# Residual and norm offset of a scan stage moved to matmuls with identities

## The chip, the cores and the metric

The kernel runs on one core of a Trainium2 chip. The metric is the device time of one execution in microseconds (us), the median of several runs.

## The reference, cut to what matters

Eight sequences of 512 tokens with 256 features go through a state-space layer and then a mixture of experts. `x` is float32 throughout.

```python
def mamba(x):                                   # 8 x 512 x 256
    x_ssm, x_gate = split(x @ in_w.T + in_b)
    x_conv = silu(causal_conv4(x_ssm) + conv_b)
    Bm, Cm = split(x_conv @ bc_w.T + bc_b)      # 16 states each
    dt = softplus(x_conv @ dt_w.T + dt_b)
    h_n = scan over the tokens: h*exp(dt*A_n) + dt*Bm_n*x_conv     # n = 0..15
    y = (sum over n of h_n*Cm_n + x_conv*D) * silu(x_gate)
    z = (y @ out_w.T + out_b) + x
    return layernorm(z) * ln_g + ln_b
x = layernorm(x + mamba(x))                     # no gain, no offset
x = layernorm(x + moe(x))                       # 8 experts, 4 per token
```

So each sequence has two norms in the scan stage. Between them the first norm's rows are scaled by `ln_g`, and `ln_b` and the old `x` are added.

## The kernel before, in words

The program has three stages: the scan stage with the routing (about 40 to 690 us of the trace, after some setup), the experts, and a last norm. The change touches the first only.

The scan stage runs in rounds, numbered -1 to 9 (`like` in the code; rounds 3 to 6 are a loop). A round has 16 steps, t = 0 to 15, one for each state. In round k several sequences are in flight: part `b` scans sequence k, part `a` prepares sequence k+1 (projection, convolution, softplus, `drive`), part `c` finishes sequence k-1 (output projection, both norms), part `d` routes sequence k-2 and starts to scatter its rows, part `e` scatters the rest of sequence k-3. Rounds 2 to 6 have all of a to d; round 1 has no routing; round 7 has no part a; round 8 has only c, d and e.

Each engine has its own instruction stream in the fixed order of its loop over t (`pe_stage1`, `act_stage1`, `dve_stage1`, `pool_stage1`), and an instruction that waits for a semaphore holds up all behind it on its engine. In step t:

- VectorE multiplies the drive by B (`weigh_inputs`, L894: `p_bu`, 1024 columns) and runs the scan (`scan`, L903: `state`). Other work of the step stands between the two: at t=2 `gate` (L911) and the ranking, at t=5 `take_counts` (L960), at t=9 `residual` (L919, four instructions), at t=11 `softplus_rest` (L867, L870), at t=13 `scan_inputs` (L877), at t=15 `drive` (L885).
- GpSimd multiplies the state of step t-1 by C (`read_state`, L1020: `read`), one step behind the scan. At t=0 it runs `add_offset` (L1053, x + ln_b in place), at t=5 `mean` of the first norm, at t=6 `power`, at t=7 `scale` (L1046, times ln_g), at t=10 `mean` of the second norm (L1030, L1031), at t=12 `power`. It also issues one or two scatters per step (L1062); these stand ahead of the other work of their step. `while_scanning` makes it wait at t=9 for the residual, at t=11 and t=13 for VectorE's softplus work.
- ScalarE computes the decays of step t+2 (`decays`, L693). At t=4 it takes the output projection out of PSUM with row sums (`take_out`, L715), at t=5 and t=11 the variances, at t=6 and t=13 it applies the norms, at t=7 the silu, at t=8 it stores dt and B/C, at t=9 softplus, at t=11 and 12 the gate's projection (`store_in`), which there stands ahead of the decays of the step.
- TensorE adds `read` of step t-2 into `p_y` (`sum_states`, L517), projects `y` at t=3 (`project_out`, L529 to L533), and counts the routed tokens at t=4 (`count`).

Results of TensorE other than `p_y` go through two PSUM banks used in turn, in the order of the list `blocks()`. TensorE waits before a block until the earlier block of that bank has been read (`block`, L465); the reader signals with `bank_read`.

## Time and profile before

| What | Value |
|---|---|
| median of 3 runs | 1407.38 us (1406.16 to 1407.46) |
| the profiled execution | 1408.09 us, of which the span of its trace is 1406.3 us |
| busy over the span | TensorE 1170.1 us, VectorE 1066.2, ScalarE 895.2, GpSimd 791.0 |
| one round in the middle (337 to 412 us) | VectorE 70.1 of 75.0 us, TensorE 62.7, GpSimd 62.5, ScalarE 50.2 |
| the experts and the last norm | from about 690 us to the end |

The 1.8 us outside the span lie before the first and behind the last instruction of the trace. A busy share over the whole span mixes the stages, so the middle row is the one for the scan stage.

### The profile page before, as it was taken

To read this page: it belongs to the slowest core of one execution; us is meant where nothing else is said; L and a number is where in the kernel's file an instruction comes from. 1 tells how busy PE (TensorE), PEld (TensorE's weight loads), DVE (VectorE), ACT (ScalarE), POOL (GpSimd) and SP (SyncE) were. 2 spreads that over 40 slices of the span, in tenths; PEclk is the share of its full clock that TensorE was granted. 3 is DMA by queue.
4 is the path that set the end of the run, shared out by engine and by line. 5 is a ranking of instruction groups with operands and counts; after the bars stand their busy time and mean duration, and the time that the engine had idled before them with its cause. 6 is when DMAs were issued, how large, how long until landed. Compare 5 with 4: busy or idle time off the path is not lost. (4 is left out here: it accounts for less than half of the span.)

```text
span 1406.3 us, 18116 instructions
## 1 busy us (share of the span) xinstructions
PE 1170.1 (83%) x5138; PEld 801.0 (57%) x5138; DVE 1066.2 (76%) x1529; ACT 895.2 (64%) x1549; POOL 791.0 (56%) x567
## 2 busy tenths in 40 slices
PE   7869697979788796761299999999999999999950
PEld 3324252524243433231188888888888888888840
DVE  2999899999999999963177777777777777777743
ACT  4765758494848576422177777776776767776744
POOL 0457568787888888977324444444444444444442
PEclk9899999999999999895599999999999999999985
DMA  2543435444444544424745655565555566555537
GB/s 92 202 151 135 152 120 196 138 170 162 161 159 146 192 153 148 157 73 153 284 140 157 158 156 156 157 155 145 144 143 147 154 159 159 156 155 157 156 40 239
DMA packets 69254, 217.13 MB, mean 154 GB/s; under 512 B 7520, under 2 KB 43232, under 8 KB 56288
## 3 DMA queue, kind: packets, MB, share of 16 engines
q1 hardware_dynamic: 29664, 167.42, 33.0%
q0 software_dynamic: 26880, 36.72, 15.4%
q10 hardware_dynamic: 12672, 12.58, 2.8%
q8 instruction: 12, 0.20, 0.1%
q14 instruction: 26, 0.21, 0.0%
HBM read 165.54 MB, written 51.15 MB: 154 GB/s over the span
## 5 line engine op out<-in xcount | busy, mean ns | idle before, releaser
L517 PE MATMUL p_y<-read,small 128*128 128x512 f32 x512 | 266.6, 653 | 88.6 <-POOL read L1020 88.3
L903 DVE TENSOR_TENSOR_SCAN state<-decay,p_bu 128x1024 f32<-128x1024 f32 x128 | 292.4, 2285 | 13.3 <-DVE p_bu L894 5.1
L1465 POOL DMA_INDIRECT total<-o_v,tok x144 | 267.3, 1856 | 44.0 <-issue 44.0
L517 PEld LDWEIGHTS p_y<-read,small 128*128 128x128 f32 x512 | 98.1, 202 | 236.0 <-POOL read L1020 136.7
L1463 POOL TENSOR_TENSOR scrap<-neg_half 128x1 f32<-128x1 f32 x36 | 14.0, 389 | 356.6 <-ACT o_v L1350 354.0
L693 ACT ACTIVATE decay<-dt,scan_rate 128x511 f32<-128x511 f32 x256 | 164.9, 710 | 22.8 <-DVE state L903 22.6
L1020 POOL TENSOR_TENSOR read<-state,bc 128x1024 f32<-128x1024 f32 x64 | 150.6, 2353 | 29.0 <-DVE p_bu L894 10.7
L1327 ACT ACTIVATE gate_v<-p_g,bias 128x512 f32<-128x512 f32 x144 | 98.3, 683 | 97.8 <-PE p_up L1276 97.7
L1337 ACT ACTIVATE ah<-a_v 128x512 fp32r<-128x512 f32 x144 | 91.2, 633 | 88.9 <-DVE a_v L1411 88.9
L1020 POOL TENSOR_TENSOR read<-state,first_wh 128x1024 f32<-128x1024 f32 x32 | 75.4, 2357 | 81.6 <-DVE p_bu L894 49.8
L1400 DVE TENSOR_SCALAR up_v<-up_v 128x512 f32<-128x512 f32 x144 | 61.3, 426 | 64.2 <-ACT up_v L1330 64.0
L1406 DVE TENSOR_TENSOR al<-a_v,ah 128x512 fp32r<-128x512 f32 x144 | 98.9, 686 | 12.8 <-ACT ah L1337 12.7
L1411 DVE SCALAR_TENSOR_TENSOR a_v<-gate_v,up_v 128x512 f32<-128x512 f32 x144 | 99.8, 693 | 4.9
L1330 ACT ACTIVATE up_v<-p_up,bias 128x512 f32<-128x512 f32 x144 | 98.0, 681 | 0.0
L1020 POOL TENSOR_TENSOR read<-state,first_wl 128x1024 f32<-128x1024 f32 x32 | 75.5, 2358 | 32.8 <-DVE first_raw L870 16.7
L894 DVE TENSOR_TENSOR p_bu<-p_u,bc 128x1024 f32<-128x1024 f32 x64 | 78.9, 1233 | 7.0 <-DVE state L903 0.5
L1292 PE MATMUL p_o<-wh,ah 128*128 128x256 f32 x288 | 82.0, 285 | 1.7 <-DVE al L1406 1.7
L1292 PE MATMUL p_o<-first_wh,ah 128*128 128x256 f32 x288 | 82.0, 285 | 0.0
L1292 PE MATMUL p_o<-wl,ah 128*128 128x256 f32 x288 | 80.6, 280 | 0.0
L1292 PE MATMUL p_o<-first_wl,ah 128*128 128x256 f32 x288 | 80.4, 279 | 0.0
L1292 PE MATMUL p_o<-wh,al 128*128 128x256 f32 x288 | 80.4, 279 | 0.0
L1292 PE MATMUL p_o<-first_wh,al 128*128 128x256 f32 x288 | 80.4, 279 | 0.0
(215 smaller groups left out, 3065.6 us busy)
## 6 DMA issues: line engine op xcount, KB each, us to landing
bc<-bc_rows SPq DMA_DIRECT2D x32, 1024.0 KB
first_raw<-in_w_experts SPq DMA_DIRECT2D x19, 1668.0 KB
raw_w<-in_w_experts SPq DMA_DIRECT2D x18, 1668.0 KB
first_wh<-bc_rows SPq DMA_DIRECT2D x16, 1024.0 KB
first_wl<-bc_rows SPq DMA_DIRECT2D x16, 1024.0 KB
first_rows<-queues SPq DMA_DIRECT2D x19, 544.0 KB
xq<-queues SPq DMA_DIRECT2D x18, 544.0 KB
queues<-read SPq DMA_DIRECT2D x9, 544.0 KB
```

Of the source, the lines that this page charges most:

```text
L517: mm = pe.matmul(p_y[h][:, :], ident[:, :], read[:, t % 4, h, :], start=False, stop=(t == SLOTS - 1))
L693: act.activation(decay[t % AHEAD][:, h, 1:LEN], dt[s.p][:, h, 1:LEN], ACT.Exp, scale=rate[:, h, t:t + 1])\
L894: dve.tensor_tensor(p_bu[:, :].rearrange("p (a b) -> p a b", a=2), p_u[:, :].rearrange("p (a b) -> p a b", a=2), of_state(t, 0), ALU.mult) ...
L903: dve.tensor_tensor_scan(flat(state[t % 4][:, :, :]), flat(decay[t % AHEAD][:, :, :]), p_bu[:, :], 0.0, ALU.mult, ALU.add).then_inc(s_stat ...
L1020: pool.tensor_tensor(read[:, t % 4, :, :], state[t % 4][:, :, :], of_state(t, 1), ALU.mult).then_inc(s_read, 1)
L1292: mm = pe.matmul(to, v[:, i, a * P:(a + 1) * P], w[t.p][:, c:c + D], start=(i == 0 and a % 2 == 0 and m == 0), stop=(i == CH - 1 and m == ...
L1327: act.activation(gate_v[i % 2][:, :], p_g[i % 2][:, :], ACT.Silu, bias=bias[t.p][:, 0, i:i + 1], scale=ALPHA)
L1330: act.activation(up_v[i % 2][:, :], p_up[i % 2][:, :], ACT.Identity, bias=bias[t.p][:, 1, i:i + 1])\
L1337: act.activation(ah[:, i, :], a_v[i % 2][:, :], ACT.Copy).then_inc(s_ah, 1)
L1406: dve.tensor_tensor(al[:, i, :], a_v[i % 2][:, :], ah[:, i, :].bitcast(F32), ALU.subtract).then_inc(s_al, 1)
L1411: dve.scalar_tensor_tensor(a_v[i % 2][:, :], gate_v[i % 2][:, :], TOP, up_v[i % 2][:, :], ALU.min, ALU.mult)\
L1465: pool.indirect_dma_start(total, bass.IndirectOffsetOnAxis(ap=tok[t.p][:, a:a + 1], axis=0), o_v[t.p][:, a, :], None, compute_op=ALU.add). ...
```

## The change

`residual`, on VectorE at t=9, and `add_offset`, on GpSimd at t=0, are gone. In their place TensorE has two new blocks `r0` and `r1` at t=9: for each of the four 128-row tiles it puts into PSUM x through the identity, ln_b through a row of ones (as three bfloat16 parts), and the scaled z through the identity. ScalarE takes these out at t=10 with the row sums, by the same function as at t=4. The second `mean` moves on GpSimd from t=10 to t=11 and now waits for both blocks to be read. `x` stays unchanged in memory, so `project_out` waits for the load of x, and the setup on VectorE splits b_out and ln_b each into three parts, where it split their difference once. GpSimd's wait for the residual at t=9 and ScalarE's wait for it ahead of the load of x are gone.

```diff
@@ blocks
-                + ["dt0", "dt1", "bc", "in2", "in3"] * a)
+                + ["dt0", "dt1", "bc"] * a + ["r0", "r1"] * c + ["in2", "in3"] * a)
@@ pe_stage1
-                pe.matmul(to, ones[0:3, :], b_parts[0:3, :], start=False, stop=False)
+                pe.matmul(to, ones[0:3, :], b_parts[0][0:3, :], start=False, stop=False)
                 if b == 0 and i == 0:
-                    pe.wait_ge(s_offset, s.n + 1)
+                    pe.wait_ge(s_x, 16 * (s.n + 1))
                 mm = pe.matmul(to, ident[:, :], x[:, 2 * b + i, :], start=False, stop=True)
             mm.then_inc(done, 1)
+        def add_residual(r, b):
+            bank, done = block(r, f"r{b}")
+            s = r.s.at(-1)
+            for i in range(2):
+                to = bank[:, i * D:(i + 1) * D]
+                pe.matmul(to, ident[:, :], x[:, 2 * b + i, :], start=True, stop=False)
+                pe.matmul(to, ones[0:3, :], b_parts[1][0:3, :], start=False, stop=False)
+                if b == 0 and i == 0:
+                    pe.wait_ge(s_scaled, s.n + 1)
+                mm = pe.matmul(to, ident[:, :], z[:, 2 * b + i, :], start=False, stop=True)
+            mm.then_inc(done, 1)
@@ (behind from_xc of t == 8)
+                if r.c and t == 9:
+                    add_residual(r, 0)
+                    add_residual(r, 1)
@@ act_stage1
-            after(act, s_residual, s.n)
-        def take_out(r, b):
+        def take_rows(r, which, b):
-            bank, done = full(act, r, f"o{b}")
+            bank, done = full(act, r, f"{'or'[which]}{b}")
             for i in range(2):
                 t = 2 * b + i
+                last = act.activation(z[:, t, :], bank[:, i * D:(i + 1) * D], ACT.Copy,
+                                      accum_out=row_sum[:, which, t:t + 1])
             last.then_inc(done, 1)
@@ (behind the decays of the step)
+                if r.c and t == 10:
+                    take_rows(r, 1, 0)
+                    take_rows(r, 1, 1)
@@ dve_setup
-        steps.then(dve.tensor_tensor(b_rest[:, :], b_out[:, :], ln_b[:, :], ALU.subtract))
+        for of, parts in ((b_out, b_parts[0]), (ln_b, b_parts[1])):
+            steps.then(dve.tensor_copy(b_rest[:, :], of))
+...
@@ dve_stage1
-                if r.c and t == 9:
-                    residual(r)
@@ pool_stage1
+            for b in range(2):
+                bank, n = r.block(f"{'or'[which]}{b}")
+                pool.wait_ge(bank_read[bank], n)
-            if r.c and t == 9:
-                pool.wait_ge(s_residual, r.s.at(-1).n + 1)
-                if r.c and t == 5:
-                    mean(r, 0)
+                if r.c and t in (5, 11):
+                    mean(r, t // 11)
-                if r.c and t == 0:
-                    add_offset(r)
-                if r.c and t == 10:
-                    mean(r, 1)
```

## Rows read from the trace of the kernel before

**Rows 1.** Windows, round 4: PE, PEld, DVE, ACT, POOL busy us; clock, DMA, GB/s.

```profile
337.00:412.00 75.00, 62.73 (x170) 28.76 (x169) 70.12 (x69) 50.21 (x89) 62.53 (x47) 0.95 0.48 164
```

**Rows 2.** Groups by line and shape, 0 to 620 us: busy us, mean ns.

```profile
L919 DVE SCALAR_TENSOR_TENSOR z<-z,x 128x256 f32<-128x256 f32 x28 | 22.6, 858 | 0.0
...
L1053 POOL TENSOR_TENSOR x<-x,small 128x1024 f32<-128x1024 f32 x8 | 16.0, 2004 | 0.0
...
L715 ACT ACTIVATE z<-p_bank 128x256 f32<-128x256 f32 x28 | 10.5, 380 | 34.5 <-PE p_bank L533 34.5
```

**Rows 3.** Timeline, round 4, steps 8 to 10: start, us, engine, tiles, [idle before].

```profile
357.01 1.23 DVE L894 TENSOR_TENSOR p_bu<-p_u,first_wh 128x1024 f32<-128x1024 f32 x1
...
360.84 1.23 DVE L894 TENSOR_TENSOR p_bu<-p_u,first_wh 128x1024 f32<-128x1024 f32 x1
...
361.63 2.37 POOL L1020 TENSOR_TENSOR read<-state,bc 128x1024 f32<-128x1024 f32 x1
...
361.98 2.31 DVE L919 SCALAR_TENSOR_TENSOR z<-z,x 128x256 f32<-128x256 f32 x1
...
368.01 1.23 DVE L894 TENSOR_TENSOR p_bu<-p_u,first_wl 128x1024 f32<-128x1024 f32 x1 [0.47 <-DVE state L903]
```

**Rows 4.** Timeline of round 4, steps 9 to 11, ScalarE's chain.

```profile
361.19 2.56 ACT L693 ACTIVATE decay<-dt,scan_rate 128x511 f32<-128x511 f32 x4
...
366.78 3.70 PE L517 MATMUL p_y<-read,small 128*128 128x512 f32 x8
...
373.36 2.56 ACT L693 ACTIVATE decay<-dt,scan_rate 128x511 f32<-128x511 f32 x4
...
375.24 2.28 DVE L903 TENSOR_TENSOR_SCAN state<-decay,p_bu 128x1024 f32<-128x1024 f32 x1
```

**Rows 5.** Timeline of round 4, steps 11 to 15, GpSimd and what it meets.

```profile
375.42 2.35 POOL L1020 TENSOR_TENSOR read<-state,first_wl 128x1024 f32<-128x1024 f32 x1 [2.28 <-DVE first_raw L870]
...
382.59 1.22 DVE L877 TENSOR_TENSOR dt<-first_raw,rest 128x1024 f32<-128x1024 f32 x1
382.66 1.21 POOL L1039 TENSOR_TENSOR neg_mean<-neg_mean,rstd 128x4 f32<-128x4 f32 x1
...
392.44 1.80 POOL L1062 DMA_INDIRECT queues<-rows,index  x1 [0.17 <-issue]
...
397.79 2.36 POOL L1020 TENSOR_TENSOR read<-state,bc 128x1024 f32<-128x1024 f32 x1
```

**Rows 6.** Timeline, first steps of rounds 4 and 5: TensorE up to the count.

```profile
325.86 1.88 PE L517 MATMUL p_y<-read,small 128*128 128x512 f32 x4
...
345.07 0.19 DVE L960 TENSOR_TENSOR place<-p_bank,base 128x32 f32<-128x32 f32 x1 [0.20 <-PE p_bank L563]
...
401.05 1.88 PE L517 MATMUL p_y<-read,small 128*128 128x512 f32 x4
...
411.48 1.03 PE L474 MATMUL p_bank<-w,y 128*128 128x256 f32 x4
...
413.19 1.03 PE L474 MATMUL p_bank<-w,y 128*128 128x256 f32 x4
```

**Rows 7.** Timeline, VectorE in round -1 and at step 11 of round 1.

```profile
32.79 1.23 DVE L867 SCALAR_TENSOR_TENSOR rest<-rest,expo 128x1024 f32<-128x1024 f32 x1 [14.70 <-ACT rest L672]
...
152.18 2.29 DVE L903 TENSOR_TENSOR_SCAN state<-decay,p_bu 128x1024 f32<-128x1024 f32 x1 [1.47 <-ACT decay L693]
```

**Rows 8.** Timeline of rounds 8 and 9, after the last scan.

```profile
621.91 1.85 PE L551 MATMUL p_bank<-small,x1t 128*128 128x8 f32 x16
...
640.06 0.43 DVE L919 SCALAR_TENSOR_TENSOR z<-z,x 128x256 f32<-128x256 f32 x1 [7.23 <-POOL z L1046]
...
644.03 0.21 POOL L1030 TENSOR_TENSOR neg_16th<-row_sum,norm_c 128x4 f32<-128x4 f32 x1
...
653.46 3.56 PE L551 MATMUL p_bank<-small,x1t 128*128 128x8 f32 x16 [0.78 <-ACT x1t L742]
...
662.89 0.19 POOL L1060 TENSOR_TENSOR scrap<-neg_half 128x1 f32<-128x1 f32 x1 [0.55 <-DVE index L997]
```

More of the change, by code:

```diff
@@ L242, in build @@
     b_part = sb("b_part", D, dt=BF16, at=one)
-    b_parts = sb("b_parts", D, dt=BF16, at=one)
+    b_parts = [sb(f"b_parts{i}", D, dt=BF16, at=one) for i in range(2)]
     dt = [sb(f"dt{i}", HALVES, LEN, at=one) for i in range(2)]
@@ L291, in build @@
     s_normed1, s_scaled, s_x1 = (sem(n) for n in ("s_normed1", "s_scaled", "s_x1"))
-    s_offset, s_t = sem("s_offset"), sem("s_t")
+    s_t = sem("s_t")
     s_route, s_rexp, s_chosen, s_index = (sem(n) for n in ("s_route", "s_rexp", "s_chosen", "s_index"))
@@ L708, in start_total @@
                           rows[s.p][:, :, 0:D]).then_inc(s_total[s.p], 16)
-        def take_out(r, b):
-            bank, done = full(act, r, f"o{b}")
+        def take_rows(r, which, b):
+            bank, done = full(act, r, f"{'or'[which]}{b}")
             for i in range(2):
                 t = 2 * b + i
-                last = act.activation(z[:, t, :], bank[:, i * D:(i + 1) * D], ACT.Copy, accum_out=row_sum[:, 0, t:t + 1])
+                last = act.activation(z[:, t, :], bank[:, i * D:(i + 1) * D], ACT.Copy,
+                                      accum_out=row_sum[:, which, t:t + 1])
             last.then_inc(done, 1)
@@ L787, in act_stage1 @@
                 if r.c and t == 4:
-                    take_out(r, 0)
-                    take_out(r, 1)
+                    take_rows(r, 0, 0)
+                    take_rows(r, 0, 1)
                 if r.a and t == 5:
@@ L822, in dve_setup @@
         last.then_inc(s_set_dve, 1)
-        steps = Steps(dve, s_raw, 0, 10)
+        steps = Steps(dve, s_raw, 0, 18)
         steps.then(dve.tensor_tensor(b_bc[:, :], b_bc[:, :], b_or_c[:, :], ALU.mult))
@@ L827, in dve_setup @@
         dve.wait_ge(s_const, SETUP)
-        steps.then(dve.tensor_tensor(b_rest[:, :], b_out[:, :], ln_b[:, :], ALU.subtract))
-        steps.then(dve.memset(b_parts[:, :], 0.0))
-        for i in range(3):
-            steps.then(dve.tensor_copy(b_part[:, :], b_rest[:, :]))
-            if i < 2:
-                steps.then(dve.tensor_tensor(b_rest[:, :], b_rest[:, :], b_part[:, :], ALU.subtract))
-            steps.then(dve.scalar_tensor_tensor(b_parts[:, :], b_part[:, :], ident[:, i:i + 1], b_parts[:, :],
-                                                ALU.mult, ALU.add))
+        for of, parts in ((b_out, b_parts[0]), (ln_b, b_parts[1])):
+            steps.then(dve.tensor_copy(b_rest[:, :], of))
+            steps.then(dve.memset(parts[:, :], 0.0))
+            for i in range(3):
+                steps.then(dve.tensor_copy(b_part[:, :], b_rest[:, :]))
+                if i < 2:
+                    steps.then(dve.tensor_tensor(b_rest[:, :], b_rest[:, :], b_part[:, :], ALU.subtract))
+                steps.then(dve.scalar_tensor_tensor(parts[:, :], b_part[:, :], ident[:, i:i + 1], parts[:, :],
+                                                    ALU.mult, ALU.add))
     def dve_setup_rest(dve):
@@ L912, in gate @@
             last.then_inc(s_y, 1)
-        def residual(r):
-            s = r.s.at(-1)
-            dve.wait_ge(s_scaled, s.n + 1)
-            for t in range(TT):
-                last = dve.scalar_tensor_tensor(z[:, t, :], z[:, t, :], 1.0, x[:, t, :], ALU.mult, ALU.add,
-                                                accum_out=row_sum[:, 1, t:t + 1])
-            last.then_inc(s_residual, 1)
         def rank_experts(r, steps):
@@ L1023, in mean @@
             s = r.s.at(-1)
-            if which == 0:
-                for b in range(2):
-                    bank, n = r.block(f"o{b}")
-                    pool.wait_ge(bank_read[bank], n)
-            else:
-                pool.wait_ge(s_residual, s.n + 1)
+            for b in range(2):
+                bank, n = r.block(f"{'or'[which]}{b}")
+                pool.wait_ge(bank_read[bank], n)
             pool.tensor_tensor(neg_16th[:, which, :], row_sum[:, which, :], norm_c[:, 0, :], ALU.mult)
```

6 lines of the change are left out of this document (removed).

## The prediction

> **What bounds the kernel now.** I read the busy time by windows first. In one round of the scan stage VectorE is busy 70.1 of 75.0 us, TensorE and GpSimd about 62.6 each, ScalarE 50.2 [rows 1]. That names VectorE, but a share does not say which wait ends last in a given step, so the timeline of one round (round 4, 320 to 402 us) is what I argue from. A step with nothing extra takes VectorE 3.83 us, from the `p_bu` at 357.01 to the one at 360.84. Step 9, with the residual, takes 7.17 us, to 368.01 [rows 3]. That is the prize: 3.34 us a round.
>
> Why so much for four instructions of 256 columns? The group's mean is 858 ns [rows 2], but the first of the four takes 2.31 us, started at 361.98, and it is released just when GpSimd's `read` of 361.63 ends, at 364.00 [rows 3]; the other three are then done within 1.4 us. VectorE stood still behind GpSimd for about 1.9 us. This is also how I treat other VectorE instructions with two operands in SBUF.
>
> Three places beside step 9 matter, because they decide how long the gain lives.
>
> - *Step 11.* ScalarE works through one chain: decays 9 and 10 from 361.19, the stores of dt, softplus with its table loads, then decays 11 and 12 from 373.36. The pair of instructions for step 11 is half of that group and ready at 373.36 + 1.28 = 374.64. VectorE's scan of step 11 started at 375.24 [rows 4]. So VectorE was only 0.6 us behind ScalarE.
> - *Steps 10 to 15 on GpSimd.* With a `read` of 2.36 us and a scatter of 1 us and its gaps, GpSimd needs about 3.6 us a step against 3.83 on VectorE. It can't make good a late start before the round ends.
> - *Step 5 of the next round.* TensorE runs without a break from the last `sum_states` of a sequence (325.86) over routing, projections and output to the count, which VectorE's L960 awaits at 345.07, idle 0.20 us for it: 19.2 us [rows 6]. So the last `read` of a sequence sets, through TensorE, when VectorE passes step 5.
>
> **The change, part by part.** All sums are made against the profiled execution, 1408.1 us with a span of 1406.3; the median of the runs is 0.7 us lower, and I subtract that by adding the differences to the median.
>
> *VectorE without the residual, step 9 to 11.* The scan of step 9 could start at 362.3 where it started at 365.3, so VectorE reaches step 11 some 3 us earlier. ScalarE's chain in between depends on the silu, on TensorE's dt blocks and on its own order, none of which is touched, and nothing in it waits for the residual. The scan of step 11 can't start before 374.7. Of 3.34 us about 0.5 is left: rounds 2 to 6. In round 1 the scan of step 11 already waited 1.47 us for its decay [rows 7]: gain 0. Bounds for one round: 0 and 3.34; I take 0.5, since it comes from the order of ScalarE's queue and not from a price.
>
> *TensorE's new blocks.* In `project_out` one tile (two products, ones, identity) takes 413.19 - 411.48 = 1.71 us [rows 6]. A 512-column group of four records takes half of 3.70 less the overlap, 1.72 us [rows 4], so a 256-column product costs 0.43. The new tile has one such product less: 1.71 - 0.43 = 1.28 us, four of them 5.1 us. They start behind the sum that begins at 366.78, at 368.5, and end at 373.6. z was scaled at 360.3, so the wait for it costs nothing here. TensorE then has 67.8 of 75 us to do. The sum of state 7 is pushed from 368.5 to 373.6; the `read` that needs its buffer comes later.
>
> *ScalarE's take.* In its queue the four copies stand behind decays 11 and 12, which end at 375.9. At 0.38 us each, with the accumulator reads between them [rows 2], they take 1.6 us, to 377.5. The gate's projection has to wait for bank r0: `in2` starts on TensorE at 376.7 and is stored at 379.2, ahead of decay 13 (ready 380.5, wanted at 385). Covered by about 4 us; without that cover a late decay would be paid in full.
>
> *GpSimd's mean at t=11.* This is the new wait. It stands ahead of the `read` of state 10 in the queue, and its condition is met at 377.5. With its two small instructions the `read` starts at 378.0 where it started at 375.42 [rows 5]: 2.6 us late. Queued behind it are the reads of states 10 to 15, the scatters and the second norm's power. From the read of state 10 to that of state 15 GpSimd took 397.79 - 375.42 = 22.4 us. In that stretch two waits of about 1 us and 0.8 us go (the 1.21 us of L1039 beside L877, the 1.80 us of a scatter beside L885; alone such instructions take 0.2 and 1.0), and two of 1.15 and 0.95 come at the same VectorE instructions, since everything on GpSimd is shifted against them. The last read ends 2.8 us later, at 402.9 instead of 400.15. Bounds: 1.5 if the new waits don't happen, 3.5 if both and more.
>
> On the same account L877, which VectorE wants to start at 382.1, meets the read of state 11 (381.5 to 383.9) and is held 1.8 us. [...]
>
> *What a late last read does.* TensorE's `sum_states` of state 15 started at 401.05 [rows 6]; there it still had the transposes before it. With the read of state 14 ending at 399.4, the sum of 14 (1.7 us, or 2.9 as it was here at the lower clock) and the transposes (1.6), it starts between 403.0 and 404.1. Plus 19.2 us this is L960. So round to round the period grows by 2.0 to 3.0 us; I take 2.4. VectorE's own lateness (0.3 at the end of the round) is hidden under that. Five rounds, 2 to 6: 12.0 us.
>
> *Round 1* has no scatters, GpSimd catches up, and VectorE may be held at L877: 0 to 1, take 0.5. *Round 7* has no softplus chain, but there GpSimd works without a gap to the end of the sequence and sets it. Only its wait for the residual goes, 0.3 us gained; VectorE's 3.3 us fall into its wait for TensorE at the end.
>
> *GpSimd without the offset.* 2.0 us eight times [rows 2], behind the last read and ahead of a read after which GpSimd waits 4.6 us for the ranking: nothing. *The waits on the load of x* replaced: x landed long before t=3: nothing. *Setup* on VectorE grows by some 4 us and is hidden in 14.70 us of idle [rows 7]; without that cover it would cost 4.
>
> *The tail, round 8.* Nothing is scanned, so the second norm is a chain of latencies. z is ready at 640.0; the residual took 1.5 us, and the mean followed at 644.03, held by scatters [rows 8]. Now r0 needs 0.43 and 1.28 us behind z, r1 2.56, then there is a take of 0.84 and some 0.4 of handovers: mean at 645.6, 1.6 us later. [...] GpSimd's queue of scatters is shifted as much as the routing, and at 662.89 it had only 0.55 us to wait for the index [rows 8], so nothing absorbs it. [...]
>
> *Sum:* 12.0 + 0.5 - 0.3 + 4.6 = +16.8 us, so 1407.4 + 16.8 = 1424.
>
> **The rivals.**
>
> *Faster: VectorE keeps its gain.* Place: step 9 to 11. If the scan of step 11 isn't held by its decay, rounds 1 to 6 give 3.34 us each, and if GpSimd's late reads then stay hidden too, 6 x 3.3 - 4.6 = 15.2 us: 1392. It decides if ScalarE finishes the softplus more than 2.5 us earlier than now. For it speaks VectorE's 93% share; against it ScalarE's unbroken chain and the 1.47 us in round 1. Already at 1.5 us of net gain a round it ends at 1404. Chance 0.12.
>
> *Rounds unchanged.* [...] Then the tail alone counts: +1.6 to +4.6, so 1409 to 1412. Chance 0.17; of this 0.07 within 0.2%.
>
> *TensorE becomes the bound.* Its 5.1 us come on top in each of seven rounds, because the sums are pushed into the projections: 7 x 5.1 = 36, 1443. Against it: it waits for GpSimd several times in steps 12 to 15, over 9 us in all. Chance 0.09.
>
> *The forecast* has 0.62, with a range of its own from 1413 (five rounds at 0.7, which is the lower bound of 1.5 less the 0.8 that TensorE gives back ahead of the sum, and a tail of 1.6) to 1430 (3.5 each, round 1 at 1, tail 4.6).
>
> **How the numbers follow.** A measurement of this kernel can tell about 0.2%, 2.8 us. Slower has the forecast, TensorE's rival and 0.10 of the unchanged rounds: 0.81. Same 0.07, faster 0.12. The range reaches from the unchanged rounds with the small tail, 1409, to 1433, a little beyond the forecast's own end; outside lie most of the faster case and of TensorE's.
>
> **What would show it.** Right: at step 11 VectorE idles for the decay of ScalarE in rounds 2 to 6; GpSimd idles several us ahead of L1030 at t=11, released by ScalarE's take; L877 grows beyond 1.22 us; VectorE idles ahead of L960 for TensorE by 1 us or more; a round takes 77 to 78 us between two L960 instead of 75.2. In round 8 the new products take twice their time. Wrong: rounds of 72 to 75 us, with the scan of step 11 released by VectorE itself, or a GpSimd that is back in step by state 13.

## The result, and the profile after

The changed kernel takes 1421.57 us, the median of 4 runs (1419.36 to 1423.15), beside 1406.77 for the kernel before in the same runs: ratio 1.0104, 95% interval [1.0086, 1.0121]. The change made the kernel 1% slower, by about what was forecast (1424, range 1409 to 1433). The profiled execution took 1423.15 us with a span of 1421.2.

In the trace after, lines are shifted: the product `p_bu` is L913, the scan L922, GpSimd's `read` L1028, the mean L1035, the three VectorE products of the softplus L886 (was L867), L896 (was L877) and L904 (was L885), the decays L708, the take of rows L729, the taking of the counts L970 (was L960).

The first view is again the windows; here one period of the scan stage, from one taking of the counts to the next. First the kernel before:

```profile
345.07:420.32 75.25, 62.98 (x170) 28.86 (x170) 70.56 (x69) 50.71 (x90) 62.78 (x47) 0.95 0.48 164
```

Then the changed kernel (start and end, length, then busy us of TensorE, its weight loads, VectorE, ScalarE and GpSimd):

```profile
351.39:428.66 77.27, 66.35 (x190) 30.95 (x190) 71.60 (x60) 52.24 (x98) 61.73 (x46) 0.98 0.45 160
```

VectorE has nine records fewer, eight of them those of the residual (the ninth lies across the edge of the first window), and is nevertheless 1.04 us *more* busy than before; the other 0.98 us of the longer period is idle time. The groups of instructions by line say which instructions grew (busy us, mean ns; before, then after):

```profile
L885 DVE TENSOR_TENSOR p_u<-dt,xc 128x1024 f32<-128x1024 f32 x8 | 14.7, 1831 | 0.6
L867 DVE SCALAR_TENSOR_TENSOR rest<-rest,expo 128x1024 f32<-128x1024 f32 x8 | 9.7, 1217 | 14.7 <-ACT rest L672 14.7
L877 DVE TENSOR_TENSOR dt<-first_raw,rest 128x1024 f32<-128x1024 f32 x8 | 9.7, 1217 | 0.0
```

```profile
L904 DVE TENSOR_TENSOR p_u<-dt,xc 128x1024 f32<-128x1024 f32 x8 | 21.6, 2699 | 0.6
L896 DVE TENSOR_TENSOR dt<-first_raw,rest 128x1024 f32<-128x1024 f32 x8 | 17.7, 2210 | 0.0
L886 DVE SCALAR_TENSOR_TENSOR rest<-rest,expo 128x1024 f32<-128x1024 f32 x8 | 14.8, 1850 | 12.9 <-ACT rest L687 12.9
```

The same three products, with the same shapes, take 20.0 us more in all. The timeline of one round shows why. Round 5, VectorE from step 9 on (start, us, and in brackets the idle time before it and who ended it):

```profile
368.88 2.29 DVE L922 TENSOR_TENSOR_SCAN state<-decay,p_bu 128x1024 f32<-128x1024 f32 x1 [0.48 <-ACT decay L708]
...
376.23 2.44 DVE L886 SCALAR_TENSOR_TENSOR rest<-rest,expo 128x1024 f32<-128x1024 f32 x1
...
381.05 2.29 DVE L922 TENSOR_TENSOR_SCAN state<-decay,p_bu 128x1024 f32<-128x1024 f32 x1 [1.24 <-ACT decay L708]
...
388.41 2.73 DVE L896 TENSOR_TENSOR dt<-first_raw,rest 128x1024 f32<-128x1024 f32 x1
...
398.52 3.57 DVE L904 TENSOR_TENSOR p_u<-dt,xc 128x1024 f32<-128x1024 f32 x1
402.01 2.27 DVE L922 TENSOR_TENSOR_SCAN state<-decay,p_bu 128x1024 f32<-128x1024 f32 x1
...
428.66 0.19 DVE L970 TENSOR_TENSOR place<-p_bank,base 128x32 f32<-128x32 f32 x1
```

And GpSimd in the same stretch:

```profile
375.22 2.36 POOL L1028 TENSOR_TENSOR read<-state,first_wh 128x1024 f32<-128x1024 f32 x1
...
383.84 0.19 POOL L1035 TENSOR_TENSOR neg_16th<-row_sum,norm_c 128x4 f32<-128x4 f32 x1 [4.30 <-ACT z L729]
...
384.14 2.35 POOL L1028 TENSOR_TENSOR read<-state,first_wl 128x1024 f32<-128x1024 f32 x1
...
387.68 2.36 POOL L1028 TENSOR_TENSOR read<-state,first_wl 128x1024 f32<-128x1024 f32 x1
...
398.63 2.36 POOL L1028 TENSOR_TENSOR read<-state,bc 128x1024 f32<-128x1024 f32 x1
...
406.52 2.37 POOL L1028 TENSOR_TENSOR read<-state,bc 128x1024 f32<-128x1024 f32 x1
```

Read them side by side, counted from the taking of the counts that opened each round (345.07 before, 351.39 after). The scan of step 11 starts at 29.66 us of its round; before it was 375.24 - 345.07 = 30.17 [rows 4, 6]. Half a microsecond is all that is left of the 3.34 us won at step 9, since the scan now waits 1.24 us for its decay. GpSimd stands idle for 4.30 us for ScalarE's take of the rows, and its read of state 10 starts at 32.75 us where it was 30.35 [rows 5, 6]. Then the read of 387.68 is under way when L896 wants to start at 388.41: 2.73 us for 1.22. The read of 398.63, that of state 13, lies over L904: 3.57 us. Before the change the same product was held by the same read, for less:

```profile
389.92 2.36 POOL L1020 TENSOR_TENSOR read<-state,bc 128x1024 f32<-128x1024 f32 x1
391.20 2.18 DVE L885 TENSOR_TENSOR p_u<-dt,xc 128x1024 f32<-128x1024 f32 x1
393.29 2.27 DVE L903 TENSOR_TENSOR_SCAN state<-decay,p_bu 128x1024 f32<-128x1024 f32 x1
```

In both kernels the product ends 1.10 us after that read ends, so the read sets when VectorE's scan of step 15 starts: at 50.62 us of its round instead of 48.22 (393.29 before), 2.4 us late, as late as the read. In holds that is the two growths, 1.51 and 1.39, less the 0.5. The round shown is 2.0 us longer in the end (77.27 against 75.25), the mean of the five 2.4.

TensorE's part, the first tile of the new blocks, and the transfer of the same lateness to its sum:

```profile
374.92 0.59 PE L541 MATMUL p_bank<-x,small 128*128 128x256 f32 x2
375.45 0.28 PE L542 MATMUL p_bank<-b_parts,ones 3*128 3x256 bf16 x1
375.65 0.70 PE L545 MATMUL p_bank<-z,small 128*128 128x256 f32 x2
376.19 0.59 PE L541 MATMUL p_bank<-x,small 128*128 128x256 f32 x2
...
408.94 1.98 PE L516 MATMUL p_y<-read,small 128*128 128x512 f32 x4 [0.70 <-POOL read L1028]
...
428.38 0.24 PE L575 MATMUL p_bank<-chosen,ones 128*128 128x32 bf16 x4
```

A tile takes 376.19 - 374.92 = 1.27 us (1.28 was forecast).

**The ledger.** Taking of the counts, rounds 2 to 7: before 195.80, 270.23, 345.07, 420.32, 495.15, 569.29; after 196.79, 273.87, 351.39, 428.66, 505.95, 582.47. The lag is 1.0, 3.6, 6.3, 8.3, 10.8, 13.2 us: 12.2 us in five rounds, and 1.0 that was there before, because the first `p_bu` of the whole kernel came at 39.90 and not 38.94. At the last read the lag is 630.61 - 617.67 = 12.9. At the second mean of round 8 it is 661.60 - 644.03 = 17.6 [rows 8], at TensorE's first product of stage 2 708.99 - 693.32 = 15.7, at the end of the span 14.9.

### The profile page after: what moved, and what is told of

It reads as the page before. It is cut to its first block and busy times, and to the rows that moved or that the text cites. A ratio compares the mean times of both kernels' runs of the same rounds, so it can differ in the third digit from the quotient of the medians.

```text
span 1421.2 us, 18451 instructions
## 1 busy us (share of the span) xinstructions
PE 1210.5 (85%) x5298; PEld 825.7 (58%) x5298; DVE 1067.1 (75%) x1475; ACT 907.7 (64%) x1613; POOL 778.9 (55%) x559
## 3 DMA queue, kind: packets, MB, share of 16 engines
q1 hardware_dynamic: 29664, 167.42, 32.7%
## 5 line engine op out<-in xcount | busy, mean ns | idle before, releaser
L516 PE MATMUL p_y<-read,small 128*128 128x512 f32 x512 | 257.4, 635 | 62.8 <-POOL read L1028 62.6
L922 DVE TENSOR_TENSOR_SCAN state<-decay,p_bu 128x1024 f32<-128x1024 f32 x128 | 292.5, 2285 | 23.5 <-ACT decay L708 15.3
L708 ACT ACTIVATE decay<-dt,scan_rate 128x511 f32<-128x511 f32 x256 | 164.8, 710 | 15.0 <-DVE state L922 14.8
L1028 POOL TENSOR_TENSOR read<-state,bc 128x1024 f32<-128x1024 f32 x64 | 150.6, 2354 | 27.2 <-DVE p_bu L913 9.2
L1028 POOL TENSOR_TENSOR read<-state,first_wh 128x1024 f32<-128x1024 f32 x32 | 75.6, 2362 | 93.0 <-DVE p_bu L913 58.8
L473 PE MATMUL p_bank<-first_raw,w 128*128 128x512 f32 x128 | 69.2, 675 | 18.1 <-ACT z L729 6.6
L913 DVE TENSOR_TENSOR p_bu<-p_u,bc 128x1024 f32<-128x1024 f32 x64 | 78.9, 1233 | 6.7
L1028 POOL TENSOR_TENSOR read<-state,first_wl 128x1024 f32<-128x1024 f32 x32 | 75.4, 2359 | 13.9 <-DVE p_bu L913 9.8
```

Of the source, the lines that this page charges most:

```text
L516: mm = pe.matmul(p_y[h][:, :], ident[:, :], read[:, t % 4, h, :], start=False, stop=(t == SLOTS - 1))
L708: act.activation(decay[t % AHEAD][:, h, 1:LEN], dt[s.p][:, h, 1:LEN], ACT.Exp, scale=rate[:, h, t:t + 1])\
L913: dve.tensor_tensor(p_bu[:, :].rearrange("p (a b) -> p a b", a=2), p_u[:, :].rearrange("p (a b) -> p a b", a=2), of_state(t, 0), ALU.mult) ...
L922: dve.tensor_tensor_scan(flat(state[t % 4][:, :, :]), flat(decay[t % AHEAD][:, :, :]), p_bu[:, :], 0.0, ALU.mult, ALU.add).then_inc(s_stat ...
L1028: pool.tensor_tensor(read[:, t % 4, :, :], state[t % 4][:, :, :], of_state(t, 1), ALU.mult).then_inc(s_read, 1)
```

## The experiments

Twelve kernels ran. "Round" is the mean of the five periods between the takings of the counts; "scan" is from the first `p_bu` to the start of the last read; "tail" from there to the second mean of round 8; all from one profiled execution, in us. The tail moves by itself: the changed kernel and e7 have the same code in round 8, and 31.0 and 29.8 us. The first `p_bu` itself came between 36.9 and 41.4 us from one execution to another, so a span says less than these columns. Ratios are to the kernel before on the same chip.

| kernel | median (runs) | ratio [95%] | round | scan | tail |
|---|---|---|---|---|---|
| before | 1406.77 (4) | 1 | 74.70 | 578.7 | 26.4 |
| changed | 1421.57 (4) | 1.0104 [1.0086, 1.0121] | 77.14 | 590.7 | 31.0 |
| e1 mean behind the read | 1413.77 (7) | 1.0051 [1.0034, 1.0067] | 75.90 | 585.3 | 30.7 |
| e2 norm a step later | 1411.03 (12) | 1.0032 [1.0021, 1.0044] | 75.05 | 579.9 | 30.0 |
| e3 VectorE's time back | 1433.25 (4) | 1.0173 [1.0141, 1.0205] | 78.97 | 602.8 | 31.7 |
| e4 before, no residual | 1402.39 (10) | 0.9970 [0.9957, 0.9984] | 74.46 | 576.9 | 26.3 |
| e5 busy tail | 1421.40 (4) | 1.0111 [1.0094, 1.0127] | 77.28 | 591.5 | 28.0 |
| e6 = e2 + e5 | 1409.45 (10) | 1.0018 [1.0006, 1.0030] | 75.12 | 580.3 | 28.9 |
| e7 x product twice | 1425.86 (4) | 1.0139 [1.0120, 1.0158] | 77.32 | 591.7 | 29.8 |
| e8 = e6 + decay first | 1403.67 (12) | 0.9981 [0.9969, 0.9993] | 74.49 | 576.2 | 29.0 |
| e9 = e8 + counts first | 1410.91 (12) | 1.0019 [1.0009, 1.0030] | 73.71 | 573.7 | 35.3 |
| e10 before, reordered | 1413.27 (6) | 1.0039 [1.0025, 1.0052] | 74.92 | 578.6 | 32.7 |
| e11 changed, counts first | 1432.74 (5) | 1.0173 [1.0158, 1.0189] | 77.80 | 593.8 | 36.5 |
| e12 = e8 + counts first in the scan | 1403.26 (12) | 0.9970 [0.9960, 0.9981] | 74.16 | 576.7 | 28.9 |

### e1: the mean behind the read

```diff
-                if r.c and t in (5, 11):
-                    mean(r, t // 11)
+                if r.c and t == 5:
+                    mean(r, 0)
@@ (behind read_state of the step)
+                if r.c and t == 11:
+                    mean(r, 1)
```

> Base is the changed kernel; only GpSimd's second mean is moved within step 11, from ahead of the read of state 10 to behind it. Theory (the queue behind the mean's wait costs the rounds): the read of state 10 no longer waits for ScalarE and starts when VectorE's softplus work of step 11 is done, at about the step's scan, so nearly all of the 4.3 us of idle time ahead of the mean shrinks to the 1 to 2 us left between that read's end and ScalarE's take; the last read of a sequence ends 1.5 to 2.5 us earlier, each of rounds 2 to 6 is 1.5 to 2.5 us shorter, in all 8 to 12 us: about 1411. [...]

Measured 1413.77, 7.8 us less than the changed kernel, a little under the 8 to 12 us that were expected; the rounds are 1.2 us shorter, not 1.5 or more. GpSimd's mean now waits 1.5 to 1.7 us behind the read instead of 4.3 ahead of it. All runs of L896 in the steady rounds are back at 1.22 us; L904 stays at 3.56:

```profile
386.90 1.22 DVE L896 TENSOR_TENSOR dt<-first_raw,rest 128x1024 f32<-128x1024 f32 x1
...
395.51 3.56 DVE L904 TENSOR_TENSOR p_u<-dt,xc 128x1024 f32<-128x1024 f32 x1
```

Only the place of a wait in GpSimd's queue was moved, so that place alone cost half of the loss.

### e2: the whole second norm a step later

```diff
@@ act_stage1
-                if r.c and t == 11:
+                if r.c and t == 12:
                     variance(r.s.at(-1), 1)
-                if r.c and t == 13:
+                if r.c and t == 14:
                     second_norm(r)
...
@@ pool_stage1
-                if r.c and t in (5, 11):
-                    mean(r, t // 11)
+                if r.c and t == 5:
+                    mean(r, 0)
@@ (behind read_state of the step)
+                if r.c and t == 12:
+                    mean(r, 1)
...
-                if r.c and t == 12:
+                if r.c and t == 13:
                     power(r.s.at(-1), 1)
```

> Base is the changed kernel; mean and variance of the second norm go to step 12 (the mean behind that step's read), its power to step 13, its application and the store of the rows to steps 14 and 15. Theory: GpSimd then waits for nothing new in rounds 1 to 7, the reads run as in the kernel before, and what is left of the change is the 0.5 us a round at step 11 gained, and the tail of round 8 lost (4.6 us at the mean, some 2 of which came back later): 1405 to 1411. Rival (products of TensorE or ScalarE's take cost the rounds): stays above 1416.

Measured 1411.03, 10.5 us less than the changed kernel and at the upper end of what was expected. The rounds are 74.8 to 75.2 us, L896 is 1.22 us and L904 2.95. This shows that the growth of the rounds came from GpSimd's wait for ScalarE's take. Whether it reached the end of the round through VectorE or through TensorE this run can't tell, since both become early again. The 0.5 us a round that was to be gained is not there: the mean round is 0.35 us longer than before the change, and L904 is held 0.77 us more than L885 was. The rest of the loss is the tail: 30.0 us against 26.4.

### e3: VectorE's time given back

Four dummy `scalar_tensor_tensor` with row sums at step 9 on VectorE in the changed kernel.

```diff
+                if r.c and t == 9:
+                    for i in range(TT):
+                        dve.scalar_tensor_tensor(z_d[:, i, :], ln_g[:, :], 1.0, ln_b[:, :], ALU.mult, ALU.add,
+                                                 accum_out=sum_d[:, i:i + 1])
```

> Base is the changed kernel; VectorE gets four instructions of the residual's kind and size back at step 9 (on constants, into a tile that nothing reads). Theory (the time that VectorE saved at step 9 had nowhere to go): the step grows by 1.5 to 3.5 us, but the scan of step 11 waited 1.2 us for its decay anyway and GpSimd sits in its wait for ScalarE; a round costs 0 to 1 us more, 0 to 6 in all: 1421 to 1427. Rival (VectorE is the bound and the gain was real, only eaten elsewhere): 1.5 to 3.3 us in each of seven rounds, 10 to 23 us more: 1432 to 1444.

Measured 1433.25, outside what was expected and inside the rival's 1432 to 1444. Part of the reason is seen in the trace of e3: two of the four instructions are held by reads, not one, so that the step grew by 5.6 us, more than the residual had cost.

```profile
368.87 2.33 DVE L1018 SCALAR_TENSOR_TENSOR z_d<-small 128x256 f32<-128x256 f32 x1
...
371.48 3.27 DVE L1018 SCALAR_TENSOR_TENSOR z_d<-small 128x256 f32<-128x256 f32 x1
...
391.99 1.21 DVE L898 TENSOR_TENSOR dt<-first_raw,rest 128x1024 f32<-128x1024 f32 x1
...
399.31 2.36 POOL L1034 TENSOR_TENSOR read<-state,bc 128x1024 f32<-128x1024 f32 x1
400.59 2.18 DVE L906 TENSOR_TENSOR p_u<-dt,xc 128x1024 f32<-128x1024 f32 x1
402.69 2.27 DVE L924 TENSOR_TENSOR_SCAN state<-decay,p_bu 128x1024 f32<-128x1024 f32 x1
```

Even so four of the five periods are only 77.0 to 77.7 us, about 0.2 more than in the changed kernel. The 5.6 us at step 9 take the place of what VectorE had lost elsewhere in the round: holds of 1.22, 1.51 and 1.39 us more than before, and the wait of 1.24 us for the decay, 5.4 us together. The first softplus product and L898 are not held at all, and yet the scan of step 15 starts at 402.69 - 351.96 = 50.73 us of its round, where it was 50.62: L906 still ends 1.10 us after the read of state 13. So it is the lateness of that read, and not the length of the holds, that makes VectorE late.

Two things make the time longer. Round 7, which has no softplus chain, takes 64.18 us instead of 61.28. And the third of the five periods is 8 us longer than its neighbours: VectorE stands still for 3.04 us ahead of its first product of a sequence (at 408.00), for which the profile names no releaser; the last read follows late, TensorE idles 2.96 us for it and goes on at the lower clock (granted 0.55 from 410 to 420 us; the 16 products of the routing take 3.42 us for 1.85), and VectorE waits 4.15 us for the counts at 437.46. The executions fall in two pairs, 1427.9 and 1429.2, 1437.3 and 1437.7, as if this came in some only. What the 3.04 us are stays open, and so e3 supports the theory by its four quiet periods only, not by its time.

### e4: the kernel before without its residual

The four instructions of the residual are left out, with the waits for them, and the second norm takes its sums from the first; the output is not the reference's.

> Base is the kernel before; the residual on VectorE is left out altogether with the waits for it (the second norm then uses the first norm's sums, and x and ln_b are not added behind it). This is the whole gain that the change could have on VectorE, with no cost anywhere. Theory: the scan of step 11 is held by the decays of ScalarE, so rounds 2 to 6 gain 0.3 to 0.6 us each, round 1 none, round 7 0.3, the tail up to 1.5: 1402 to 1405. Rival (3.3 us a round are there to be had): 6 to 7 rounds at 3.3, 1384 to 1388.

Measured 1402.39: 4 us less, not 20. All of VectorE's 3.34 us a round is taken away here, and nothing is added anywhere. This is where it goes; trace of e4, round 4:

```profile
368.08 2.44 DVE L866 SCALAR_TENSOR_TENSOR rest<-rest,expo 128x1024 f32<-128x1024 f32 x1
...
372.90 2.29 DVE L902 TENSOR_TENSOR_SCAN state<-decay,p_bu 128x1024 f32<-128x1024 f32 x1 [1.25 <-ACT decay L693]
```

Having come early, VectorE meets a read at L866 (2.44 us for 1.22) and then waits 1.25 us for ScalarE's decay. Without the hold that wait would have been longer by as much. The gain at step 9 is gone by step 11 in a kernel in which TensorE, GpSimd and ScalarE have nothing more to do.

### e5: a TensorE kept busy in the tail

```diff
                 if b == 0 and i == 0:
+                    if not r.b:
+                        for _ in range(9):
+                            pe.matmul(p_y[0][:, :], ident[:, :], xc[0][:, 0, :], start=True, stop=True)
                     pe.wait_ge(s_scaled, s.n + 1)
```

> The changed kernel, with nine further products of 512 columns in the last round only (round 8, which has no scan), ahead of the wait for the scaled rows; they are thrown away. In the trace of the changed kernel the granted clock was 0.50 in the last stretch before stage 2 and the new products there took 1.2 us instead of 0.7. Theory (the clock's half level costs the tail some 3 us, because each ScalarE take waits for its products): the new products of round 8 take 0.3 to 0.7 us each again, and the second mean of round 8 stands 2 to 3 us earlier against the end of the scan; total 1418 to 1420. Rival (ScalarE and the scales of GpSimd set the tail whatever the clock is): the products are shorter, the mean stands where it stood, total 1421 to 1422. The rounds before round 8 are as in the changed kernel in both.

In the changed kernel TensorE waits 7.57 us and then works at half the clock (granted 0.50 from 653.0 to 659.7 us), up to the last tile at 659.67 (TensorE, round 8):

```profile
653.01 1.22 PE L545 MATMUL p_bank<-z,small 128*128 128x256 f32 x2 [7.57 <-POOL z L1051]
654.02 1.06 PE L541 MATMUL p_bank<-x,small 128*128 128x256 f32 x2
...
661.60 0.19 POOL L1035 TENSOR_TENSOR neg_16th<-row_sum,norm_c 128x4 f32<-128x4 f32 x1 [3.43 <-ACT z L729]
```

In e5 it comes to the same products out of other work (granted 1.00 from 651 to 656 us):

```profile
643.53 7.99 PE L546 MATMUL p_y<-xc,small 128*128 128x512 f32 x18
651.36 0.59 PE L548 MATMUL p_bank<-z,small 128*128 128x256 f32 x2
651.79 0.59 PE L541 MATMUL p_bank<-x,small 128*128 128x256 f32 x2
...
656.79 0.20 POOL L1038 TENSOR_TENSOR neg_16th<-row_sum,norm_c 128x4 f32<-128x4 f32 x1 [0.44 <-ACT z L732]
```

The pair on x takes 0.59 us instead of 1.06, and the tail is 28.0 us instead of 31.0. So in these two executions the tail's growth of 4.6 us is 1.7 us of work and 3.0 us of clock. The 3.0 are not a fixed price: in e7, with the same code in this place, the products are back at full speed some 2 us earlier (the pair on z takes 0.70 us at 657.80, where the changed kernel's at 657.66 takes 1.22), and the tail is 29.8. The median, though, did not move (1421.40, each median uncertain by some 2 us), and lies where the rival had it (1421 to 1422): between the mean and TensorE's first product of stage 2, 1.6 of the 3.0 us are given back (47.4 us in the changed kernel, 49.0 in e5), which leaves less than these runs can tell. The mechanism of the theory is seen in the rows; its gain in the time is not shown.

### e6: e2 and e5 together

> The norm's second half a step later on GpSimd and VectorE (as in e2), and the nine further products in round 8 (as in e5). If the two costs are independent the time is that of e2 less the gain of e5: 1407 to 1409, against 1411.03 for e2. The rounds should be 75.0 to 75.2 us as in e2. Rival (in e2 the tail is already bound by GpSimd's steps): no less than e2's 1411.

The edit moves ScalarE's part of the norm, as in e2, and none of VectorE's. Measured 1409.45, 1.6 us less than e2, the intervals overlapping, and between theory and rival. The tail is 28.9 us against 30.0. It is the base of what follows.

### e7: the products with x twice

```diff
+                if r.b:
+                    pe.matmul(to, ident[:, :], x[:, 2 * b + i, :], start=True, stop=True)
                 pe.matmul(to, ident[:, :], x[:, 2 * b + i, :], start=True, stop=False)
```

> The changed kernel with the product of x and the identity issued twice for each tile in rounds 0 to 7: TensorE has some 0.4 us a tile, 1.7 us a round, more to do, and the output is the same. Theory (TensorE's new blocks lie under cover: in round 5 the blocks are done at about 379 us and ScalarE takes them at 382): the rounds grow by 0 to 0.5 us each, total 1421 to 1425. Rival (TensorE's own time is what the rounds have grown by; the counts then wait for it): the rounds grow by 1.7 us each, six of them, total 1431 to 1434.

The rounds are 77.32 us against 77.14, so 1.7 us of further work on TensorE in each of them is hidden, and the rival of a TensorE that sets the round by its amount of work is refuted. The median of 1425.86 is 4.3 us above the changed kernel's and 0.9 above the expected range; the profiled executions differ by 1.3 us only. Where the rest is, they do not show.

### e8: the decay ahead of the logarithm

```diff
@@ act_stage1 (between the exponential and the logarithm of the softplus)
+            if r.b:
+                decays(r.s, 9 + AHEAD - 2)
...
-                if r.b and t < SLOTS - AHEAD + 2:
+                if r.b and t < SLOTS - AHEAD + 2 and not (r.a and t == 9):
                     decays(r.s, t + AHEAD - 2)
@@ dve_stage1 (softplus_rest ends at its wait for the logarithm)
+        def add_log(r):
+
+            s = r.s.at(1)
             dve.wait_ge(s_log, s.n + 1)
...
+                if r.a and t == (12 if r.b else 10):
+                    add_log(r)
@@ pool_stage1
-            if r.a and t == 11:
+            if r.a and t == 12:
                 pool.wait_ge(s_sum, r.s.at(1).n + 1)
```

> e6, and on ScalarE the decays of scan step 11 are put ahead of the logarithm of the softplus; VectorE adds the logarithm one step later, and GpSimd waits for the sum one step later. Theory (the scan of step 11 waits for its decay, which stood behind the logarithm, 1.2 us of idle VectorE in the changed kernel, and this is where the time that VectorE got back at step 9 was lost): the scan of step 11 starts up to 2.5 us earlier in rounds 1 to 6, the rounds are 72.5 to 74.5 us instead of 75.1, total 1392 to 1404. Rival (the reads and scatters of GpSimd, some 3.6 us a step, are the bound already, or the wait only moves to the next decay): rounds shorter by less than 0.5 us, total 1404 to 1409.

Measured 1403.67, 5.8 us less than e6 and 0.2% less than the kernel before. But the three periods in the middle are still 75.07 to 75.09 us, which is what the rival said; of the 4.1 us that the scan column lost, 1.3 and 1.4 lie in the first and the fifth period. The trace of e8 shows that both were right in part. At step 11 the scan follows at once, with no wait for the decay:

```profile
368.82 2.45 DVE L891 SCALAR_TENSOR_TENSOR rest<-rest,expo 128x1024 f32<-128x1024 f32 x1
371.19 2.27 DVE L930 TENSOR_TENSOR_SCAN state<-decay,p_bu 128x1024 f32<-128x1024 f32 x1
...
399.25 1.23 DVE L921 TENSOR_TENSOR p_bu<-p_u,first_wl 128x1024 f32<-128x1024 f32 x1
401.86 1.29 DVE L938 TENSOR_TENSOR y<-p_y,sg 128x512 f32<-128x512 f32 x2 [1.38 <-PE p_y L516]
403.45 0.19 DVE L945 TENSOR_TENSOR lg<-p_bank,small 128x32 f32<-128x32 f32 x1 [0.30 <-PE p_bank L566]
...
419.05 0.19 DVE L978 TENSOR_TENSOR place<-p_bank,base 128x32 f32<-128x32 f32 x1 [1.21 <-PE p_bank L578]
```

VectorE does the `p_bu` of 399.25, which is step 2 of the next sequence, 3.1 us earlier than e6 (402.33): 1.24 us by the decay, and 1.73 because the drive now comes ahead of the read of state 13 and takes 1.23 us where e6 has 2.96. It then gives back 1.38 + 0.30 + 1.21 = 2.9 us in waits for TensorE. TensorE had waited 4.61 us for a read at 392.49, did two sums at the lower clock (6.64 us for 8 products that take 3.70 at full speed; the granted clock was 0.66 between 390 and 400 us), and was busy without a gap from there to the counts. GpSimd's last read is no earlier than in e6 (53.19 us of its round against 53.03). In rounds 3 to 7 only e8 has VectorE standing still for TensorE at the counts by over 1 us time after time; otherwise it came once in e1 (1.08 us) and once in e3 (4.15).

### e9 to e12: the counts ahead of the output projection

TensorE's block of the counts moves from step 4 to 3, ahead of `project_out`, and VectorE's taking of them from step 5 to 4 (in the order of the banks too).

```diff
-        return (... ["o0", "o1"] * c + ["cnt"] * d ...)
+        return (... ["cnt"] * d + ["o0", "o1"] * c ...)
+                if r.d and t == 3:
+                    count(r)
                 if r.c and t == 3:
                     project_out(r, 0)
                     project_out(r, 1)
-                if r.d and t == 4:
-                    count(r)
...
-                if r.d and t == 5:
+                if r.d and t == 4:
                     take_counts(r, route_steps)
```

e9 does this to e8, e11 to the changed kernel, e10 does this and the reordering of the decays to the kernel before; e12 is e9 with the old order in the rounds that scan nothing.

> e8, with TensorE's block of the counts put ahead of the output projection (step 3 in place of 4) and VectorE's taking of the counts at step 4 in place of 5. In e8 VectorE was 3.1 us earlier at step 15 than in e6 (start of that step's product 399.25 against 402.33) and then waited for TensorE: 1.38 us for the sum, 0.30 for the logits, 1.21 for the counts. Theory (with VectorE relieved TensorE's stretch of solid work from the sum to the counts ends the round, and the counts' wait is given back if their block stands ahead of the projection): the rounds are 73.6 to 74.4 us instead of 75.07, total 1396 to 1401. Rival (TensorE's whole work in a round is the bound, the wait moves to the sum or to the reads): rounds within 0.3 us of e8's, total 1402 to 1405.

> The kernel before, with the same two reorderings as e9: the decays of scan step 11 ahead of the softplus's logarithm, with VectorE's addition of it one step later, and the block of the counts ahead of the output projection. VectorE has the residual of 3.3 us at step 9 again and TensorE none of the new blocks. [...] Rival (the reorderings are what gained in e8, and the change of this case gives nothing even then): as much below 1406.6 as e9, total 1396 to 1401.

> The changed kernel with the block of the counts put ahead of the output projection, and nothing else. Its VectorE waited 0.2 to 0.4 us for the counts. Theory (the late last read made VectorE itself late, through the holds of its products by GpSimd's reads, and TensorE arrives just at the same time): rounds 76.9 to 77.4 us, total 1419 to 1422. Rival, which is the prediction's own step (TensorE's sum, late by the last read, is what VectorE waits for at the counts): rounds shorter by over 1 us, total 1411 to 1416.

> e9, with the counts' block ahead of the output projection only in the rounds that scan; in round 8 the order is e8's. In e9 five rounds took 368.56 us against 372.44 in e8 (3.9 us less), but in round 8 TensorE stood 3.23 us ahead of the counts for the ranks of VectorE, with the output projection queued behind them, and went on at the half clock; round 8's second mean came at 649.30 against 644.62. Theory (that wait is the whole of e9's loss): round 8's second mean stands at 640 to 642, total 1398 to 1402 against 1403.67 for e8. Rival (the loss of e9 has another cause, such as the bank that the counts share): total 1404 or more.

e9's rounds are 73.71 us, as expected, and its time is 1410.91, 7 us *more* than e8's, for the tail grew by 6.3 us. Its trace, TensorE in round 8:

```profile
623.36 0.19 PE L574 MATMUL p_bank<-chosen,before 128*128 128x40 bf16 x1 [3.23 <-DVE chosen L958]
623.38 0.25 PE L578 MATMUL p_bank<-chosen,ones 128*128 128x32 bf16 x4
623.49 2.05 PE L473 MATMUL p_bank<-w,y 128*128 128x256 f32 x4
```

With no scan to fill the time, the counts wait 3.23 us for VectorE's ranking, the output projection stands in the queue behind them, and then runs at half the clock (granted 0.50 from 623.4 to 625.6 us; 2.05 us for the four products that take 1.03 at full speed). e12 takes that away: the tail is e8's again (28.9), so this was the cause of e9's loss. But e12's rounds are 74.16 us and not 73.7, its second mean stands at 644.14 where 640 to 642 was expected, and the time, 1403.26, misses the expected 1398 to 1402 by a little. Two of its periods are 1.2 us longer than e9's for a reason that the runs don't settle.

e11 bears on the prediction's own step. Its rounds are 77.80 us, longer and not shorter, and outside both ranges, as is its time. VectorE waits for TensorE nowhere in these rounds, and they are no shorter for it: so a late TensorE was not what made the round longer by itself; the two engines arrive together, each late by the same reads. The test is not a clean one, as the move brings a wait of its own, which may be the 0.66 us more. The counts' bank is taken by VectorE at 426.53, and TensorE's third tile of the projection, which uses the same bank, waits for it (TensorE, e11):

```profile
426.96 1.13 PE L473 MATMUL p_bank<-w,y 128*128 128x256 f32 x4 [1.11 <-issue]
```

The rest of e11's 11 us is, as in e9, the tail (36.5). e10 gains nothing in its rounds (74.92 against 74.70, scan 578.6 against 578.7) and pays 6.3 us in the tail, so that its 1413.27 lies above the 1402 to 1407 that were expected and above the rival's range. The same two reorderings on top of e6 give rounds shorter by 1.4 us (e9). So the pair is worth something in the rounds only where VectorE has been relieved. For the decays alone this is not shown: no run has them on the kernel before without the counts' move. Of the versions measured, the change with its norm a step later and the decays ahead (e8, e12) is the fastest that computes the reference, 0.2 to 0.3% below the kernel before. That the kernel before could not have the same from e12's order was not tested.

## Why the prediction was right, and which steps failed

*VectorE's gain dies at step 11.* Right, and by the size: 0.5 us was forecast to be left, 30.17 - 29.66 = 0.51 is. e4 shows it alone. The prediction named only ScalarE's decay as the place, and that is what sets it. A good part of the lost time falls one instruction earlier, where VectorE's L886, too early by 3 us, runs into a read (2.44 us for 1.22), but without that hold the wait for the decay would be longer by as much. Even the 0.51 us does not shorten the round, since the read of state 13 holds the drive later on.

*GpSimd's mean waits ahead of the read.* Right, and the cause of the rounds' growth by e1 and e2. The read of state 10 is 2.4 us late (2.6 forecast), that of state 15 2.4 us (2.8 forecast); the two take as long apart as before, 22.4 us, where the prediction had new waits of GpSimd outweigh the old ones by 0.3.

*What carries this lateness to the next round.* This step failed. The prediction has TensorE's sum of the last state carry it, VectorE standing idle 1 us or more for TensorE at the counts, while "VectorE's own lateness (0.3 at the end of the round) is hidden under that". VectorE idles at most 0.4 us there, and is itself 2.4 us late at its scan of step 15: L896 was held as forecast (1.5 us; 1.8 forecast), but L904 is held 2.3 us, 1.4 us more than before, where the forecast 0.3 comes out only if the 0.95 us that L885 had been held goes away. The product ends 1.10 us after the read of state 13 in every steady round of all kernels but e8, e9 and e12. Where that puts the scan of step 15 the length of the round follows, in us: e4 47.7 and 74.5, before 48.2 and 74.7, e2 48.5 and 75.1, e1 49.1 and 75.9, changed 50.6 and 77.1, e3 50.7 and 77.3 (the scan in the third period, the round as in the table, for e3 the mean of its four quiet periods). The amount came out right (2.44 us a round against 2.4) because both engines hang on the same reads and are equally late, so that it did not matter that the wrong one was named; in that the forecast was lucky. TensorE's path is there too: in e8, where VectorE is 3 us ahead, it alone keeps the rounds at 75.07 us.

*TensorE's new blocks are covered.* Right: 1.27 us a tile, and e7 adds 1.7 us more for 0.2 us a round. With VectorE relieved further (e8) VectorE waits 2.9 us a round for TensorE; that stretch begins with TensorE's own wait of 4.61 us for a read, and whether the new blocks have a part in it no run tells apart.

*ScalarE's take* delayed `in2`, but no decay behind it is waited for (VectorE's waits for decays are 0.48 us at step 9, 1.24 at step 11 and at most 0.22 elsewhere); covered, as forecast.

*Round 1*: 0.5 us was forecast. The lag of 1.0 us at the counts of round 2 is as large as that of the very first `p_bu`, so round 1 cost nothing. The start-up, not VectorE's longer setup, brought that 1.0: VectorE still idles 12.9 us for L886 in the first round. Between executions the first `p_bu` moves by more than this.

*Round 7*: -0.3 forecast, 12.9 - 13.2 = -0.2 measured. *The tail*: +4.6 forecast, 17.57 - 12.94 = +4.6 measured, and the split into 1.6 of work and 3 of clock is what e5 shows (1.7 and 3.0), for one execution of each. The 4.6 of the forecast was the author's estimate, and no run of the kernel before shows it: what its trace shows are the 16 products of the routing, 3.56 us at 653.46, where the granted clock was 0.50, and 1.85 us at 621.91, where it was 1.00 [rows 8]. In the changed kernel the products behind TensorE's 7.57 us of idling ran at a granted clock of 0.50: the same pair takes 1.06 us, about the twice that was forecast, against 0.59 in e5, where the clock was 1.00.

*What was missed*: behind the tail 2.7 us come back (17.6 at the mean, 14.9 at the end). The prediction said that nothing would absorb it. In the sum this stands against the 1.0 of the start-up: 16.8 was forecast and 14.8 measured, between the medians.

*The rivals.* Faster: refuted by e4, whose whole gain without any added work is 4 us. Rounds unchanged: became nearly true in e2 (75.05 us against 74.70), once the wait was put elsewhere. TensorE as the bound by its work: refuted by e7.

## What to carry to other kernels

Work taken from the busiest engine is worth what the next wait on that engine leaves of it: look at the margin of the next two or three instructions behind it before counting a gain. Work that is moved brings a new wait into some engine's queue, and its place in that queue decides: here a norm one step later, a TensorE kept busy in the tail and the decays ahead of the logarithm took 18 us off a change that had cost 15. A wait that is harmless in a full round can be the bound in the last ones, so an order for the steady state is worth giving to the steady state alone (e9 and e12).

## What the runs showed that was not expected

A VectorE product of 1.22 us can be held by a `read` of GpSimd even where its record starts first. L886, L896 and L904 of the round shown start at 376.23, 388.41 and 398.52, the reads beside them at 375.22, 387.68 and 398.63; the three end at 378.67, 391.14 and 402.09, which is 1.09, 1.10 and 1.10 us after the ends of those reads, while the reads took their usual 2.36 us. L904 is ahead by 0.11 us in the records and is held by the whole read.

With a longer lead it goes the other way. In e8, at step 11 of round 1:

```profile
147.56 1.22 DVE L891 SCALAR_TENSOR_TENSOR rest<-rest,expo 128x1024 f32<-128x1024 f32 x1
147.74 3.27 POOL L1038 TENSOR_TENSOR read<-state,first_wl 128x1024 f32<-128x1024 f32 x1 [1.29 <-DVE p_bu L921]
```

Here the product takes its 1.22 us and the read 0.9 us more than usual. In the traces of all fourteen kernels the three products (the first of the softplus, `dt` and the drive) start ahead of an overlapping read 40 times: 25 times by 0.10 to 0.19 us, and VectorE is held, and 15 times by 0.17 to 0.92 us, and GpSimd is held, its reads taking 2.52 to 3.27 us. So by these rows it is always GpSimd that is held from a lead of 0.20 us in the records on; at 0.17 to 0.19 us it is either of the two, so there the records' starts don't tell which.
